# Two mixture-of-experts dispatch tables: where their unused rows are cleared, in a two-layer attention and experts kernel on one Trainium2 core

## What is computed

```python
x = x + L0_xattn(layernorm(x), ctx, ctx, mask, mask, ...)   # 16 heads of 8, a key is masked where its bit differs from the query's
x = x + L0_ffn(layernorm(x), ...)                           # 8 experts, top 2, relu, 128 -> 512 -> 128
x = x + L1_xattn(layernorm(x), ctx, ctx, ...)               # 16 heads of 64, causal
x = x + L1_ffn(layernorm(x), ...)                           # 8 experts, top 2, silu gate, 128 -> 352 -> 128
```

## Time and profile before

| | |
|---|---|
| median of 3 runs | 838.76 us (831.14 to 841.51) |
| the profiled execution | 843.45 us |
| its span, first to last instruction | 841.5 us |
| mean granted clock of TensorE | 0.884 |
| TensorE busy | 694.4 us, 83% |
| VectorE, ScalarE, POOL busy | 480.5, 395.8, 374.7 us |
| written to device memory | 11.58 MB |
| first tile of layer 0's experts on TensorE | 274.96 us after the span's start |
| first tile of layer 1's experts on TensorE | 729.18 us |

### The profile page before, as it was taken

How to read it: one execution, slowest core, us unless ns; L and a number is a source line. 1 busy time by engine, 2 the same in 40 slices (tenths; PEclk the granted TensorE clock), 3 DMA queues, 4 the chain that set the end, 5 groups by cost and what they waited for, 6 DMA issues and landing times.

```text
span 841.5 us, 16921 instructions
## 1 busy us (share of the span) xinstructions
PE 694.4 (83%) x5142; PEld 525.2 (62%) x5142; DVE 480.5 (57%) x1326; ACT 395.8 (47%) x1115; POOL 374.7 (45%) x579
## 2 busy tenths in 40 slices
PE   2998888988870899948999999899999786399990
PEld 1666665655540788837667767676767554299980
DVE  6756667667414455533765676666665662366664
ACT  2145555545431566625675565656565540133320
POOL 6411465442343355540444555555545463245551
PEclk9999788778555899978999999999999996599995
DMA  9000000000003121231000000000101100212215
GB/s 300 20 13 8 32 26 27 26 26 14 15 13 114 46 56 54 63 118 55 27 21 19 8 27 7 27 11 21 35 21 32 29 12 13 61 46 57 58 46 150
DMA packets 38523, 36.86 MB, mean 44 GB/s; under 512 B 5742, under 2 KB 34676, under 8 KB 38166
## 3 DMA queue, kind: packets, MB, share of 16 engines
q1 hardware_dynamic: 28230, 19.10, 8.0%
q0 software_dynamic: 5616, 12.11, 4.4%
q10 hardware_dynamic: 4592, 4.59, 1.9%
HBM read 25.11 MB, written 11.58 MB: 44 GB/s over the span
## 4 chain that ended last, share of the span: by engine, by line
PE 46%; issue 14%; POOL 13%; DVE 13%; ACT 6%; DMA 5%; SPq 3%; POOLq 0%; DVEq 0%; ACTq 0%
PE ps L601 7%; PE ps L622 5%; PE ps L433 5%; PE ps L464 5%; POOL work L1634 4%; PE ps L406 4%; POOL dispatch L1569 3%; PE ps L612 3%; DVE work L1077 3%; DVE mx L1353 2%; POOL work L1633 2%; ACT work L946 2%; PE ps L638 2%; DMA work<-dispatch 2%; PE ps L684 1%
## 5 line engine op out<-in xcount | busy, mean ns | idle before, releaser
L1077 DVE TENSOR_REDUCE work<-ps 128x2 f32<-128x512 f32 x128 | 86.8, 687 | 68.4 <-PE ps L438 60.2
L946 ACT ACTIVATE work<-ps,nb 128x128 f32<-128x128 f32 (+1 forms) x256 | 104.3, 420 | 42.5 <-DVE nb L1360 38.1
L1617 POOL DMA_INDIRECT results<-work,dsti x78 | 76.6, 982 | 91.8 <-DVE work L1318 31.2
L827 ACT ACTIVATE work<-ps 128x512 f32<-128x512 f32 x128 | 74.5, 599 | 81.1 <-PE ps L433 77.6
L1633 POOL TENSOR_TENSOR work<-work,rc 128x256 f32<-128x256 f32 x64 | 39.4, 615 | 152.9 <-DVE rc L1368 152.8
L601 PE MATMUL ps<-w_up,chib 128*128 x351 | 87.6, 378 | 1.9
L1353 DVE TENSOR_REDUCE mx<-ps 128x6 f32<-128x768 f32 x64 | 61.1, 954 | 39.4 <-PE ps L671 38.9
L1569 POOL DMA_INDIRECT dispatch<-pay,sloti x64 | 65.6, 1026 | 34.4 <-DVE sloti L1149 18.1
L622 PE MATMUL ps<-w_dn,work 128*128 x546 | 74.1, 276 | 1.9 <-DVE work L1321 0.9
L638 PE MATMUL ps<-hl,ra 128*128 128x256 f32 x384 | 63.3, 306 | 7.6 <-ACT work L922 4.5
L433 PE MATMUL ps<-ra 32*128 32x256 f32 x256 | 62.5, 394 | 8.1 <-DVE work L1077 5.4
(11 more groups left out here) (162 smaller groups left out, 1444.6 us busy)
## 6 DMA issues: line engine op xcount, KB each, us to landing
work<-dispatch SPq DMA_DIRECT2D x78, 64.5 KB, 1.8
stage<-in_wgu ACTq DMA_DIRECT2D x16, 176.0 KB
ct<-in_ctxT SPq DMA_DIRECT2D x16, 128.0 KB, 2.6
w_dn<-in_w SPq DMA_DIRECT2D x1, 2048.0 KB, 9.9
stage<-in_w POOLq DMA_DIRECT2D x8, 256.0 KB, 3.1
ybuf<-results SPq DMA_DIRECT2D x16, 128.0 KB, 2.5
work<-results SPq DMA_DIRECT2D x8, 256.0 KB, 5.0
stage<-in_w1p POOLq DMA_DIRECT2D x3, 512.0 KB, 4.3
```

What stands on the lines that cost most here:

```text
L946: ac = act.activation(p1[:, pp % 2, e, cols], bk[:, cols], ACT.Exp, scale=SC1, bias=nb1[:, pp % 2, e, t:t + 1], accum_out=rs1[:, pp % 2, e ...
L1077: ve.tensor_reduce(mx0[:, g // 2, :, 32 * j + 26 + g], ps[:, n % 2, :].rearrange("p (t n) -> p t n", t=QT), AX, ALU.max).then_inc(s["a_max ...
L1617: po.indirect_dma_start(yc[l], bass.IndirectOffsetOnAxis(ap=dsti[:, k:k + 1], axis=0), ye[:, k, :], None, bounds_check=TOPK * T - 1, oob_i ...
```

## The change

1. A table is cleared whole, ahead of time. A region shrinks from 2176 to 2048 rows (`REGION = T`), so a table has 16,512 rows, 8.52 MB.
2. Table 0 is cleared by ScalarE's queue: behind the first two `low_base`, ahead of `batches(body0)`, ScalarE waits for `blank_ready` and issues 4 DMAs of 4096 rows and one of 128.
3. Table 1 is cleared by SP's queue: after each of the context loads of layer 0 comes a clear of 2048 rows, after the last one two more, and the 128 rows behind.
4. `ends_i`, its VectorE operation, the 8 reads and clears and the waits for them go, in both layers. POOL waits for the clears ahead of the first send of each layer.
5. The third split of `w1p` (`weights_high(2)`, `weights_low(2)`) moves from ahead of `experts(0)` into it, behind the copies of tile 8.

```diff
-REGION = T + P
+REGION = T
@@ SyncE @@
-            sp.wait_ge(s["blank_ready"], 1)
-            for l in range(2):
-                sp.dma_start(xs[l][ROWS - P:ROWS, :], blank[:, :]).then_inc(s[f"slots_blank{l}"], 16)
             sp.dma_start(w_dn[:, :], a["w2"]).then_inc(s["w2_in"], 16)
...
+            def clear(k):
+                src = blank[:, None, :].broadcast_to([P, T // P, PAY])
+                sp.dma_start(xs[1][k * T:(k + 1) * T, :].rearrange("(p n) d -> p n d", p=P), src).then_inc(s["slots_blank1"], 16)
+
+            sp.wait_ge(s["blank_ready"], 1)
             for k in range(2, B):
                 context(0, (0, k))
+                clear(k - 2)
+            clear(B - 2)
+            clear(B - 1)
+            sp.dma_start(xs[1][ROWS - P:ROWS, :], blank[:, :]).then_inc(s["slots_blank1"], 16)
...
-                sp.wait_ge(*after(l, "ends_ready", 1))
-                for e in range(E):
-                    row = sp.value_load(ends_i[0:1, l, e:e + 1], min_val=e * REGION, max_val=e * REGION + T)
-                    sp.dma_start(xs[l][bass.ds(row, P), :], blank[:, :]).then_inc(s[f"slots_blank{l}"], 16)
-                sp.wait_ge(s[f"slots_blank{l}"], 16 * (1 + E))
                 sp.wait_ge(*after(l, "table_ready", 1))
@@ ScalarE @@
             low_base((0, 0), 1)
+            act.wait_ge(s["blank_ready"], 1)
+            for k in range(4):
+                dst = xs[0][2 * k * T:2 * (k + 1) * T, :].rearrange("(p n) d -> p n d", p=P)
+                act.dma_start(dst, blank[:, None, :].broadcast_to([P, 2 * T // P, PAY])).then_inc(s["slots_blank0"], 16)
+            act.dma_start(xs[0][ROWS - P:ROWS, :], blank[:, :]).then_inc(s["slots_blank0"], 16)
             batches(body0)
...
                             act.activation(he[:, u % 2, :], ps[:, 1 + u % 2, :], ACT.Copy).then_inc(s["e_hcopy"], 1)
+                            if u == 8:
+                                weights_high(2)
...
-            for w in range(3):
-                act.wait_ge(s[f"st_in{w % 2}"], 16 * (E // 2 + 1 + w // 2))
-                act.activation(w1p[:, w, 0, :], stage[:, w % 2, :], ACT.Copy).then_inc(s["wl_hi"], 1)
+            weights_high(0)
+            weights_high(1)
@@ VectorE @@
-                ve.tensor_copy(ends_i[:, l, :], total).then_inc(s["ends_ready"], 1)
...
+                            if u == 8:
+                                weights_low(2)
...
-            for w in range(3):
-                ve.wait_ge(s["wl_hi"], w + 1)
-                ve.tensor_tensor(w1p[:, w, 1, :], stage[:, w % 2, :], w1p[:, w, 0, :], ALU.subtract).then_inc(s["wl_split"], 1)
+            weights_low(0)
+            weights_low(1)
@@ GpSimd @@
+                    if no(b) == 0:
+                        po.wait_ge(s[f"slots_blank{l}"], 16 * (E + 1) if l else 16 * 5)
...
-            po.wait_ge(s["slots_blank0"], 16)
             batches(body0)
```

More of the change, by code:

```diff
@@ L147, in program @@
         before = sb("before", [1, NTILE])
-        ends_i = sb("ends_i", [1, 2, E], I32)
         tile_e = sb("tile_e", [1, 2, WORDS], I32)
@@ L221, in program @@
                      hot_done=B, hots_done=B, seen_done=2 * (B - 1), diff_done=1, exp_done=1, wts_den=1, wts_one=1, wts_done=1, pfx_psum=B,
-                     hp_done=B, slot_ready=B, sent0=256, sent1=256, table=17, table_ready=1, ends_ready=1,
+                     hp_done=B, slot_ready=B, sent0=256, sent1=256, table=17, table_ready=1,
                      e_x=NTILE, e_xhi=NTILE, e_xlo=NTILE, e_h=NTILE, e_hs=0, e_hcopy=NTILE, e_ht=NTILE,
@@ L871, in _, with weights_high @@
             low_base((0, 0), 1)
+            act.wait_ge(s["blank_ready"], 1)
[3 more added lines that the diff above has]
+            act.dma_start(xs[0][ROWS - P:ROWS, :], blank[:, :]).then_inc(s["slots_blank0"], 16)
             batches(body0)
             weight_exp(0)
+            def weights_high(w):
+                act.wait_ge(s[f"st_in{w % 2}"], 16 * (E // 2 + 1 + w // 2))
+                act.activation(w1p[:, w, 0, :], stage[:, w % 2, :], ACT.Copy).then_inc(s["wl_hi"], 1)
             def experts(l):
@@ L1274, in _, with weights_low @@
             batches(body0)
+            def weights_low(w):
+                ve.wait_ge(s["wl_hi"], w + 1)
+                ve.tensor_tensor(w1p[:, w, 1, :], stage[:, w % 2, :], w1p[:, w, 0, :], ALU.subtract).then_inc(s["wl_split"], 1)
             def experts(l):
@@ L1661, in _ @@
             po.wait_ge(s["seen_set"], 2)
-            po.wait_ge(s["slots_blank1"], 16)
             for k in range(B):
```

## The result

| | before | after |
|---|---|---|
| median | 837.96 us (831.14 to 841.51, 4 runs) | 877.69 us (875.43 to 889.62, 4 runs) |
| ratio, 95% interval | 1 | 1.0475 (1.039 to 1.0561) |
| profiled execution | 843.45 us | 877.85 us |

The change makes the kernel 39.7 us slower by the medians, 34.4 us by the two profiled executions; the profiled one of the kernel before lies 5.5 us above its median. Forecast were 15.2 us and a range up to 861.

The account below looks back on a forecast made before the run. No engine is full; engines work in step, and clears end the stretch before the experts. Terms -7.8 + 0.2 + 0 + 21.8 + 1.0 = +15.2 us on the median 838.76 gave 854.0 us, 1.8% slower, range 832 to 861.

Parts of the forecast that it names:

- Added: table 0 on ScalarE's queue: Start of the program: open descriptors hold ScalarE's clear issues until 47.6 us, delaying everyone by 21.8 us; full stall given 0.60.
- lower bound: Rival of slower stores or clock: 268 GB/s, so 926 rows take 28.5 us, +2.1; 861 us in all, chance 0.09.
- `values0` term: TensorE's `values0` at the program's start begins at 49.0 instead of 27.20 because ScalarE is held: +21.8 us.
- The rival of queued commands: Whole commands wait outside the row count, each freeing ScalarE 7.3 us earlier: 846.7 with one, 839.4 with two; chance 0.14.
- The 1.0 us for the clock: After some 20 us idle in the stall, TensorE must regain its clock: +1.0 us, bounds 0 to 4.
- Nothing later gives it back: The 21.8 us shift from the start stays to the end, since engines in step pace the batches.
- The savings: Clears behind the regions removed ahead of the experts: 4.8 us in layer 0, 3.0 in layer 1, together -7.8 us.
- the send's landing: Layer 0's last send, issued at 265.10, lands in 2.14 us, as an indirect DMA of 128 rows to the results does.
- The split: Third split of `w1p` moved into the expert stage: +0.2 us, as VectorE has about half its time free; 2.3 without cover.
- Table 1 on SP: Eight clears of 2048 rows between layer 0's context loads, 3.6 us each: cost 0, bounds 0 to 1 us.
- POOL's wait: Wait ahead of the first send: costs nothing, since the clears land near 51 us and that send was at 95.86.

Follow-up runs that it names:

- Aligned rows in the kernel: The changed kernel with table rows of 576 bytes in place of 516, same DMAs at the same places: 856.04 us, ratio 1.025 to the kernel before.
- the stores alone: A program of DMAs without the computation, six stores of 4096 rows one after another: 17.8 us at 516-byte rows, 8.9 at 512.
- the second of two: The changed kernel with table 0 cleared by two DMAs (8192 and 8320 rows) on ScalarE's queue instead of five: 857.04 us, one run.
- the version on SP: The changed kernel with table 0 cleared by SP ahead of and between context loads, w_dn loaded behind: 827.23 us, ratio 0.9927; again 829.42 us, 0.993.

## Why the prediction was wrong

The sign and the mechanism were right, the size was not: 39.7 us measured, 15.2 forecast.

**The step that failed** is in "Added: table 0 on ScalarE's queue": "The rate of saturated stores of 512-byte rows is 290 GB/s, so one row of 516 bytes on each engine, 8256 bytes, takes 28.5 ns". A rate of rows of 512 bytes was carried over to rows of 516. Measured: 142 GB/s, 58 ns. The same text took 268 GB/s as its lower bound, "The clears between the stages moved 169 GB/s at a share of 0.63". That row was misread: of the 0.68 MB in its 4 us most belongs to the third load of `w1p`, 0.52 MB, which was issued at 267.47 and landed 4.2 us later. No row before showed the rate of these stores; it is half of that bound. The hold was then forecast to end at 47.6 and ended at 74.7; the `values0` term was +21.8 and measured +50.3. Aligned rows in the kernel (hold until 50.3 where 48 was expected) and the stores alone (17.8 against 8.9 us) show that this one number was wrong, and that the rest of the step holds to 2 or 3 us.

**Right in it:** that open descriptors hold an issue, and about how many. At 142 GB/s an engine writes 17.2 rows a us. With the first data an estimated 1 us after the issue, the second issue was let go with some 124 of 256 rows an engine open, the last with 100 of 1024, the second of two with 91 of 512; the prediction had 106. The rival of queued commands fell: no further command waited outside.

**The 1.0 us for the clock** had the wrong sign, and "Nothing later gives it back" was wrong too. The stall was partly given back: the third and fourth context loads are 50.4 and 49.2 us late, the fifth to eighth only 41. Context loads of the changed kernel on SP, then of the kernel before:

```profile
99.96 0.33 SPq L317 DMA_DIRECT2D ct<-in_ctxT  x1
...
118.64 0.33 SPq L317 DMA_DIRECT2D ct<-in_ctxT  x1
```

```profile
50.76 0.33 SPq L322 DMA_DIRECT2D ct<-in_ctxT  x1
...
77.64 0.33 SPq L322 DMA_DIRECT2D ct<-in_ctxT  x1
```

One batch took 26.9 us before and 18.7 after. The grouped matmuls of that batch, before and after:

```profile
L464 PE MATMUL ps<-work 128*32 128x256 f32 x64 | 7.1, 590 | 0.0
```

```profile
L463 PE MATMUL ps<-work 128*32 128x256 f32 x64 | 4.3, 385 | 0.0
```

The same 64 matmuls at 590 and 385 ns: the profile's clock column reads 1.00 in both stretches, yet the same work takes 1.53 times as long in the first. Two stretches of the kernel before, by the clock column and by these matmuls (shortest, median, longest in ns):

```profile
52.00:64.00 12.00, 11.46 (x75) 7.37 (x65) 5.72 (x10) 5.29 (x11) 2.70 (x4) 1.00 0.03 9
L464 PE MATMUL ps<-work x32: 634/634/637, 51.4 to 60.7; 128*32 128x256 f32 x32
...
160.00:168.00 8.00, 8.00 (x52) 5.46 (x48) 4.40 (x12) 3.73 (x7) 3.43 (x5) 0.50 0.04 13
L464 PE MATMUL ps<-work x20: 634/634/634, 159.7 to 167.7; 128*32 128x256 f32 x20
```

Where the column reads 0.50, the lower level (1.2 GHz), they take 634 ns; from 104 to 110 us, where it reads 1.00, the upper (2.4 GHz), the median is 379. So for much of the first stretch TensorE ran at its lower level, which the column does not show there, and in the second at its upper. Why it reached the upper level sooner behind the hold no run shows. This batch gives back 8.2 us of the 12.6; by the end of the attention the lateness is 37.7 us (`sloti`, 259.91 and 297.63).

**The savings** were forecast as 4.8 + 3.0 us, measured 2.7 + 2.9. In layer 0 the term that failed is the send's landing, taken as 2.14 us; it takes 4.28. The load of the first tile, 1.81 us, was as forecast. Removing the clears' wait was right both times.

**The split** was forecast at +0.2 and cost nothing: TensorE has no gap around tile 8 in the changed kernel. **Table 1 on SP** costs nothing by itself, but beside a slow clear of table 0 it does, through POOL's wait; that was the second miss. It is hidden here: the last clear landed at 83.5 us and the first send starts at 136.93, 41 us late for the hold's sake.

**The accounts** of the two profiled executions: +50.3 for the hold, -12.6 regained in the attention, -2.7 at the first transition, +2.6 in the experts and the second attention, -2.9 at the second, -0.6 behind: 34.1 us, the difference of the spans. The 5.6 us of savings alone agree with the 5 to 6 us of the version on SP. What makes up the +2.6 is not shown.

**Two rules, weighed again.** The Trainium skill's page "DMA: Bandwidth & Descriptors", section "Issuing engines are not separate DMA queues", calls an issue usually small relative to the DMA: true of the first clear (0.6 us), not of any behind it (8.7 to 15.8 us). The Trainium skill's page "DMA: Bandwidth & Descriptors", section "How a descriptor splits into AXI transactions", says that a descriptor that does not start at a multiple of 256 bytes is split differently and fetches bytes it doesn't use. The 512-byte rows at a pitch of 516 agree in kind, with 17.4 against 8.9 us, but the doubling is measured here for stores and is more than that account gives: in its units of 32 bytes an aligned row of 512 takes 16 and any other at most 24, an estimate from that page. And three in four of the 576-byte rows don't start at a multiple of 256 either, yet lose nothing: 9.6 us for 12% more bytes than the 512-byte rows store in 8.9. What these stores need is less than that; which alignment is enough, below 64 bytes, was not tried.

## What to carry to other kernels

Issue a large DMA as one instruction, or from an engine that nobody waits for: here every issue behind clears of 4096 rows or more, however small, held its sequencer until some 91 to 124 descriptors an engine were left open. Take a transfer's rate from a row of the same size and alignment, sustained for as long as the transfer; rows at 516-byte steps were stored at half the rate of rows at 512, and long pieces from a replicated source at nearly three times the rate of single 516-byte rows. When a wait replaces work that was done in place, price the landing of what it waits for together with all that shares the engines.

## What the runs showed of the hardware that was not expected

- Stores to device memory: 4096 rows in 17.8 us at 516 bytes, 8.9 at 512, 17.4 for 512 bytes at a pitch of 516, 9.6 at 576; 516-byte rows in 6.4 us when they go in pieces of 16.5 KB.
- One DMA of 16,512 rows occupies its issuer 0.64 us; a DMA of 128 rows behind four of 4096 occupies it 15.8 us.
- Early in the program matmuls of one shape take 590 or 385 ns on the mean while the clock column shows 1.00 for both; later they take 634 ns where it shows 0.50 and 379 where it shows 1.00.
- The last send before the experts takes 3.6 to 4.3 us to land in layer 0 (2.27 in one trace) and 2.3 to 2.5 in layer 1, with neither the third weight load nor VectorE's splits as the reason.
